# Column sums of the output weights by TensorE from the raw weights, the first z from the keys, token fetches in four pieces

## What is computed

```python
W0 = eye(32)                              # for every sequence and head
def step(W, kv):
    kc, vc = kv
    z = kc @ W                            # the first z is kc itself
    grad = kc.T @ ((z - vc) * inv_n)
    return (W - grad, z)
_, zs = scan(step, W0, (k_chunks, v_chunks))      # 32 chunks
out = (zs - mean(zs)) * rsqrt(var(zs) + eps) * ln_gamma + ln_beta
x = layernorm(x + out @ Wo.T)
```

## Time and profile before

| | |
|---|---|
| median of three runs | 689.74 us |
| the profiled execution | 689.75 us |
| its span | 687.9 us |
| TensorE busy | 662.7 us (96%) |
| VectorE busy | 431.3 us (63%) |
| ScalarE busy | 299.3 us (44%) |
| GpSimd busy | 294.6 us (43%) |

### The profile page before, as it was taken

One profiled execution on the slowest core, in us unless ns is written; L12 is line 12 of the kernel. 1 busy time (PEld: TensorE's weight loads), 2 busy tenths in 40 slices (PEclk: granted clock), 3 DMA queues, 4 the chain that ended last, 5 costly groups with the idle time before them and its releaser, 6 DMA issues.

```text
span 687.9 us, 16521 instructions
## 1 busy us (share of the span) xinstructions
PE 662.7 (96%) x6880; PEld 531.3 (77%) x6880; DVE 431.3 (63%) x750; ACT 299.3 (44%) x520; POOL 294.6 (43%) x308
## 2 busy tenths in 40 slices
PE   9889999999999999999999999999999999999994
PEld 8666777777777777887887888888887888888883
DVE  5796766776844455498956544554456267676555
ACT  5543534445554432431033556655667442142132
POOL 0747657767735531011006335442552244726232
PEclk9999999999999999999999999999999999999998
DMA  8212333331442531100065578666647765414212
GB/s 288 81 35 61 90 106 97 96 111 52 144 139 78 158 114 61 45 1 0 3 244 147 152 286 299 207 228 251 221 159 263 252 191 164 123 65 132 64 77 91
DMA packets 65854, 92.47 MB, mean 134 GB/s; under 512 B 16816, under 2 KB 31920, under 8 KB 65776
## 3 DMA queue, kind: packets, MB, share of 16 engines
q1 hardware_dynamic: 60096, 72.76, 31.8%
q0 software_dynamic: 5680, 18.62, 9.6%
HBM read 67.56 MB, written 23.79 MB: 133 GB/s over the span
## 4 chain that ended last, share of the span: by engine, by line
PE 57%; DVE 20%; POOL 9%; issue 7%; ACT 4%; DMA 2%; DVEq 0%; POOLq 0%; ACTq 0%
PE bank L1311 7%; PE zbank L1274 6%; PE wbank L1274 6%; PE bank L1079 6%; PE zbank L1187 5%; PE bank L1134 5%; PE wbank L1187 4%; PE bank L1200 3%; DVE x L1470 3%; POOL xg L1840 2%; DMA xg<-yd,SI 2%; PE zbank L1287 2%; DVE x L1518 2%; PE bank L1187 2%; PE zbank L1097 2%
## 5 line engine op out<-in xcount | busy, mean ns | idle before, releaser
L1802 POOL TENSOR_TENSOR xl<-RAW,xh 128x1024 fp32r<-128x1024 f32 x23 | 55.4, 2410 | 124.1 <-ACT xh L1669 124.0
L1685 ACT ACTIVATE ah<-sg 128x512 fp32r<-128x512 f32 x48 | 30.3, 632 | 158.9 <-DVE sg L1460 158.9
L1815 POOL DMA_INDIRECT xg<-x1d,idxu x39 | 42.0, 1077 | 70.0 <-DVE idxu L895 41.3
L1450 DVE TENSOR_TENSOR GL<-RAW,GH 128x1024 fp32r<-128x1024 f32 x42 | 50.3, 1223 | 11.0 <-ACT GH L1664 9.6
L1462 DVE TENSOR_TENSOR al<-sg,ah 128x512 fp32r<-128x512 f32 x48 | 35.3, 735 | 33.5 <-ACT ah L1685 33.5
L1200 PE MATMUL bank<-xh,ah 128*128 128x512 f32 x128 | 51.2, 400 | 1.7 <-DVE x L1470 1.1
L1840 POOL DMA_INDIRECT xg<-yd,SI x32 | 34.7, 1086 | 38.1 <-DVE x L1518 23.9
L1200 PE MATMUL bank<-xh,al 128*128 128x512 f32 x128 | 50.0, 390 | 0.0
L1200 PE MATMUL bank<-xl,ah 128*128 128x512 f32 x128 | 49.9, 390 | 0.0
L1079 PE MATMUL bank<-xh,GH 128*128 128x512 f32 x112 | 47.6, 425 | 2.1 <-DVE vst L1366 1.3
L1460 DVE TENSOR_TENSOR sg<-sg,zbank 128x512 f32<-128x512 f32 x22 | 15.1, 685 | 53.3 <-PE zbank L1274 36.4
(11 more groups left out here) (306 smaller groups left out, 1762.3 us busy)
## 6 DMA issues: line engine op xcount, KB each, us to landing
RAW<-in_wgu SPq DMA_DIRECT2D x13, 1024.0 KB, 6.7
yd<-RAW SPq DMA_DIRECT2D x39, 256.0 KB, 4.5
RAW<-in_wsgu SPq DMA_DIRECT2D x14, 512.0 KB, 5.2
RAW<-in_wd SPq DMA_DIRECT2D x13, 512.0 KB, 5.7
xr<-in_xT SPq DMA_DIRECT2D x16, 256.0 KB, 4.6
x<-in_xtok SPq DMA_DIRECT2D x16, 256.0 KB, 3.1
x1d<-x SPq DMA_DIRECT2D x16, 256.0 KB, 2.2
RAW<-in_wsd SPq DMA_DIRECT2D x8, 512.0 KB, 4.5
```

What stands on the lines that cost most here:

```text
L1450: e.tensor_tensor(GL[:, w % 2, k:k + 2, :], gate_raw(w, k), GH[:, w % 2, k:k + 2, :].bitcast(F32), ALU.subtract).then_inc(*mark("low", "g" ...
L1802: e.tensor_tensor(DL[:, w % 2, :, :], draw[:, raw_of(w), :, :], DH[:, w % 2, :, :].bitcast(F32), ALU.subtract).then_inc(*mark("low p", "d" ...
L1815: e.indirect_dma_start(place(s), None, x1d, bass.IndirectOffsetOnAxis(ap=idxu[:, LINES[s]:LINES[s] + 1], axis=0)).then_inc(*mark(f"dma xg{ ...
```

## The change

- The steps `ones`, `wo bias rows`, `wo gamma` and `wo sum` go. A step `wo scales` on ScalarE writes gamma/512 and beta, each repeated over 128 columns, into rows 8 and 9 of `x1`.
- `wo mean` and `wo bias` are four fp32 products each, of those scales with the raw weights. `wo mean` stands directly behind the projections of block 0, `wo bias` directly behind z 1 (they were behind z 1 and behind z 2).
- `wo centre` is one `scalar_tensor_tensor` a quarter, gamma * weights - mean, which reads the mean from PSUM and writes rows 4 to 7 of `x1`; it, `wo high` and `wo low` come two half steps earlier. The copy to `colsum` goes.
- z 0 is no longer multiplied: VectorE takes keys minus values (`first`, 128x256, in `za`) and spreads its first half by the mask; ScalarE spreads the second. The first `v load` and the start copy of `W` go. All four `x high` of block 1 stand behind one another ahead of it.
- `fetch tokens` issues four DMAs of 256 KB; for block 0 two at n = 43 and two at n = 44, with nothing between on SP.
- `rope_of` uses row 11 of `x1` for blocks 1 to 3; `fetch row` 11 waits for key piece (3, 6), 7 and 15 for none, and row 4 for the low output weights.

```diff
-    do("ones")
+    do("wo scales")
...
-    do("wo bias rows")
-    for k in range(4):
-        do("wo gamma", k)
+    do("wo mean", left[6])
     do("w start")
...
-    do("v load", 0)
...
+        do("x high", 1, k, ("proj", 0, 7))
         if k < 2:
-            do("x high", 1, k, ("proj", 0, 7))
             do("x low", 1, k)
...
             if n % 2 == 0:
-                do("z", n // 2)
+                if n:
+                    do("z", n // 2)
                 do("residuals", n // 2)
-                for k in (2, 3) if n == 0 else ():
-                    do("x high", 1, k, ("proj", 0, 7))
...
-        if n == 43:
-            do("fetch tokens", 0, None)
+        if n in (43, 44):
+            do("fetch tokens", 0, None, (2 * n - 86, 2 * n - 85))
...
         if n == 2:
-            do("wo mean", left[7])
-            left[7] = ("wosum", "mean")
-            later.insert(0, [("wo sum", "bias")])
+            do("wo bias", left[7])
+            left[7] = ("wosum", "bias")
+        for k in range(4):
+            if n == 1 + k // 2:
+                do("wo centre", k)
+            if n == 2 + k // 2:
+                do("wo high", k)
+            if n == 3 + k // 2:
+                do("wo low", k)
...
-            return rope if u % 4 == 0 else (kS[:], (zT[:], x1[:, 7, :], x1[:, 15, :], x1[:, 15, :])[q])
+            return rope if u % 4 == 0 else (kS[:], x1[:, 11, :] if q else zT[:])
...
-                    e.dma_start(XL[q % 2][:].bitcast(F32), chunked(x1td[:, q * 512:q * 512 + 512])).then_inc(*mark(f"dma xr{q % 2}", q))
+                    for k in ks:
+                        e.dma_start(XL[q % 2][:, k, :].bitcast(F32), x1td[128 * k:128 * k + 128, q * 512:q * 512 + 512]).then_inc(*mark(f"dma xr{q % 2}", q, k))
...
+                    what, b = ("mean", 6) if step == "wo mean" else ("bias", 7)
+                    e.wait_ge(*on("wo scales"))
+                    e.wait_ge(*on("dma wo"))
                     e.wait_ge(*on(*a[0]))
-                    e.matmul(bank[6][:], onesr[:].bitcast(F32), sums[:, 0, :], start=True, stop=True).then_inc(*mark("sums", "bias"))
+                    for k in range(4):
+                        t = e.matmul(bank[b][:], woscale[b - 6][:, k, :], wor[:, k, :], start=(k == 0), stop=(k == 3))
+                    t.then_inc(*mark("sums", what))
...
-                    e.tensor_tensor(wor[:, k, :], wor[:, k, :], colsum[:], ALU.subtract).then_inc(*mark("woprep", "centre", k))
+                    if k == 0:
+                        e.wait_ge(*on("sums", "mean"))
+                    e.scalar_tensor_tensor(out=woc[:, k, :], in0=wor[:, k, :], scalar=gams[:, k:k + 1], in1=bank[6][:], op0=ALU.mult, op1=ALU.subtract).then_inc(*mark("woprep", "centre", k))
...
+                    if n == 0:
+
+                        e.wait_ge(*on("kturn", 0, 6))
+                        e.wait_ge(*on("vturn", 0, 7))
+                        e.wait_ge(*on("dma small"))
+                        e.tensor_tensor(first.rearrange("p (g x) -> p g x", g=4), KK[:, 0, 1, :].rearrange("p (g x) -> p g x", g=4)[:, :, 0:64],
+                                        vst[0][:, 0, :].rearrange("p (g x) -> p g x", g=4), ALU.subtract).then_inc(*mark("first"))
...
+                elif step == "wo scales":
                     e.wait_ge(*on("dma small"))
-                    for k in range(4):
-                        e.activation(wor[:, k, :], wor[:, k, :], ACT.Copy, scale=gams[:, k:k + 1]).then_inc(*mark("woscaled", "g", k))
+                    for j, (s, c) in enumerate(((gams, 1.0 / 512), (bets, 1.0))):
+                        t = e.activation(woscale[j], s[:].unsqueeze(2).to_broadcast([128, 4, 128]), ACT.Copy, scale=c)
+                    t.then_inc(*mark("wo scales"))
```

More of the change, by code:

```diff
@@ L166, in stages @@
             later.append([("x low", 1, k)])
-    later.append([("wo sum", "mean")])
     def gate(w, q):
@@ L222, in shared @@
         yield from gate(3, 0)
-        do("fetch tokens", 2, ("gate", 3, 0, 1, 1))
+        do("fetch tokens", 2, ("gate", 3, 0, 1, 1), range(4))
         yield from down(2, 1)
@@ L308, in stages @@
         if n == 2:
-            do("wo mean", left[7])
-            left[7] = ("wosum", "mean")
-            later.insert(0, [("wo sum", "bias")])
-        if n == 4:
-            do("wo bias", left[6])
-            left[6] = ("wosum", "bias")
-        for k in range(4):
-            if n == 3 + k // 2:
-                do("wo centre", k)
-            if n == 4 + k // 2:
-                do("wo high", k)
-            if n == 5 + k // 2:
-                do("wo low", k)
+            do("wo bias", left[7])
[7 more added lines that the diff above has]
+                do("wo low", k)
+        if n == 4:
+            left[6] = ("woprep", "centre", 3)
         if n == 34:
@@ L469, in stages @@
         if j == JOBS - 1:
-            do("fetch tokens", 3, row_left[1])
+            do("fetch tokens", 3, row_left[1], range(4))
         if j:
@@ L598, in program @@
         W = part(pa, "late", "W", [2, 256])
-        onesr = part(pa, "late", "onesr", [128], F32R)
         mask = part(pa, "late", "mask", [64])
@@ L604, in program @@
         wgx = part(pa, "late", "wgx", [4, 16], F32R)
-        part(pa, "late", "padl", [176])
+        part(pa, "late", "padl", [304])
         vst = (sb(pa, "vst0", [8, 256]), vst1)
@@ L616, in program @@
         pa.close()
-        wor, wob, sums = x1[:, 12:16, :], x1[:, 4:8, :], x1[:, 8:12, :]
+        first = za[:].rearrange("p m x -> p (m x)")[:, 0:256]
+        wor, woc = x1[:, 12:16, :], x1[:, 4:8, :]
+        woscale = [x1[:, 8 + j, :].rearrange("p (k n) -> p k n", k=4) for j in range(2)]
         rope = (shuf[:], t1[:])
@@ L962, in sync @@
                 elif step == "fetch tokens":
-                    q, after = a
+                    q, after, ks = a
                     if after:
@@ L1371, in vector @@
                         e.tensor_tensor(xl[:, k, :], xr[:, k, :], xh[:, k, :].bitcast(F32), ALU.subtract).then_inc(*mark("low", "x", q, k))
-                elif step == "wo sum":
-                    what, = a
-                    src, at, made = (wor, 2, "g") if what == "mean" else (wob, 0, "b")
-                    e.wait_ge(*on("woscaled", made, 3))
-                    e.tensor_tensor(sums[:, at, :], src[:, 0, :], src[:, 1, :], ALU.add)
-                    e.tensor_tensor(sums[:, at + 1, :], src[:, 2, :], src[:, 3, :], ALU.add).then_inc(*mark("woprep", what, "two"))
-                    e.wait_ge(*on("woprep", what, "two"))
-                    e.tensor_tensor(sums[:, at, :], sums[:, at, :], sums[:, at + 1, :], ALU.add).then_inc(*mark("woprep", what))
                 elif step == "wo centre":
                     k, = a
-                    e.wait_ge(*on("wosum", "mean"))
-                    e.tensor_tensor(wor[:, k, :], wor[:, k, :], colsum[:], ALU.subtract).then_inc(*mark("woprep", "centre", k))
+                    if k == 0:
+                        e.wait_ge(*on("sums", "mean"))
+                    e.scalar_tensor_tensor(out=woc[:, k, :], in0=wor[:, k, :], scalar=gams[:, k:k + 1], in1=bank[6][:], op0=ALU.mult, op1=ALU.subtract).then_inc(*mark("woprep", "centre", k))
                 elif step == "wo low":
@@ L1584, in scalar @@
                     n, = a
+                    r4 = r[:, n // 2 % 2, n % 2, 256:512].rearrange("p (a b e) -> p a b e", a=4, b=2)
+                    if n == 0:
+                        e.wait_ge(*on("first"))
+                        for b in (0, 1):
+                            t = e.activation(r4[:, :, b, :], first[:, 128:256].rearrange("p (a e) -> p a e", a=4), ACT.Copy, scale=mask[:, 32 * b:32 * b + 1])
+                        t.then_inc(*mark("resid a", 0))
+                        continue
                     e.wait_ge(*on("z", n, 1))
@@ L1604, in scalar @@
                     e.activation(xh[:, k, :], xr[:, k, :], ACT.Copy).then_inc(*mark("high", "x", q, k))
-                elif step == "wo mean":
-                    e.wait_ge(*on("sums", "mean"))
-                    e.activation(colsum[:], bank[7][:], ACT.Copy, scale=1.0 / 512).then_inc(*mark("wosum", "mean"))
                 elif step == "wo bias":
                     e.wait_ge(*on("sums", "bias"))
-                    e.activation(bias[:], bank[6][:], ACT.Copy).then_inc(*mark("wosum", "bias"))
+                    e.activation(bias[:], bank[7][:], ACT.Copy).then_inc(*mark("wosum", "bias"))
                 elif step == "wo high":
```

44 lines of the change are left out of this document (12 added, 32 removed).

## The result

The changed kernel takes 688.37 us (median of 20 runs, 687.85 to 689.72), the kernel before on the same chip 690.35 us (20 runs, 689.03 to 693.3): ratio 0.9974, 95% interval 0.9966 to 0.9982. The span of the profiled run fell by 1.4 us.

A forecast was written before the change was run, and what follows sets the result against it. TensorE, nearly full behind 58 us, was taken to bound the kernel, so only waits in front could be won: -0.47, +2.58, +0.43, -1.60, -1.40 and -1.74 sum to -2.2, giving 687.5 us, range 686.3 to 689.4.

The forecast's parts named there:

- The walk through the queue: TensorE's starts carried from 27.81 us to the first output product: 53.27 instead of 55.48, 2.2 us earlier.
- the reason given: At z 2: ScalarE's W copy queues behind the bias copy until 42.3 us, so z 2 waits some 0.4 us.
- The 0.43 us a record: In both sums on TensorE: fp32 records start 0.43 us apart, eight taking 3.44 us; upper bound 0.53 apart.
- The cover of the mean sum: Behind block 0's projections: the mean costs little, lying where TensorE waited; g 0 still 0.47 us earlier.
- the bias sum in the path: Behind z 1: four products instead of one stand fully in the path, making g 1 2.1 us later than before.
- Pieces at nothing: Token fetches in four issues cost nothing; the last has 3.2 us of cover, the other two more.
- pieces land later: Rival at the token fetches: a second spread of 2.8 us passes the cover, leaving +0.2, 689.9 us; chance 0.06.
- VectorE's sizes: In front: keys minus values at most 0.42 us, low output weights at most 2.34 a pair; no wait at g 0.
- reaches the end almost whole: Behind the first 58 us TensorE is nearly full, so the 2.2 us earlier start carries to the end.
- a stall goes as well: Rival inside z at 183.06 us: TensorE's 0.91 us standstill vanishes too; -3.1, 686.6 us; chance 0.10.
- bytes and place are the same: Argument against the 0.91 us standstill at 183.06 us vanishing: the first 1 MB fetch keeps its bytes and place.
- given back: Rival behind 58 us: a VectorE or GpSimd step loses its slack, half the gain lost; -1.0, 688.7 us; chance 0.14.

The follow-up runs named there:

- experiment 7: The changed kernel with two of the mean sum's four fp32 products left out; 688.0 us, ratio 0.9964 to the kernel before.
- experiment 8: The changed kernel with two of the bias sum's four fp32 products left out, which changes routing and expert tiles; 684.35 us, ratio 0.9917 to the kernel before.
- experiment 3: The changed kernel with each token fetch as one DMA again; 688.61 us, ratio 0.9963 to the kernel before.
- 1: The changed kernel run again unaltered for a second trace; 688.56 us, ratio 0.9972 to the kernel before.
- 9: The changed kernel with its bias sum two steps later, behind g 2; 690.19 us, ratio 1.0004 to the kernel before.
- 10: The changed kernel with its warm-up of ten fp32 products made 5 wide and 31 narrow, 52 records more; 688.95 us, ratio 0.9986 to the kernel before.
- 11: The changed kernel with its warm-up of ten fp32 products made 7 wide and 16 narrow, 26 records more; 688.76 us, ratio 0.9983 to the kernel before.
- 12: The changed kernel with 13 narrow fp32 products added ahead of the x1 turn near 214 us; 688.69 us, ratio 0.9982 to the kernel before.
- experiment 4: The kernel before with only the first z taken from the keys; 690.28 us, ratio 1.0 to the kernel before.
- 5: The kernel before with the first z from the keys and four unused fp32 products ahead of the projections; 689.89 us, ratio 0.9997 to the kernel before.
- 6: The changed kernel with z 0 multiplied as before and one DMA per fetch, column sums alone; 689.08 us, ratio 0.9975 to the kernel before.

## Why the prediction was right

**The walk through the queue** came out within 0.12 us at every step: the mean's end (31.3 forecast; the second projection behind it starts at 31.56, which is 31.33 and one spacing), g 0 at 32.80 (32.75), z 1 at 35.16 (35.13), g 1 at 39.58 (39.55), z 2 at 42.47 (42.35) with its wait of 0.46 (0.4) for the reason given, g 2 at 46.20 (46.13), g 3 at 50.93 (50.89), the output product at 53.21 (53.27). The 0.43 us a record, the term with the widest bounds, held: 0.86 a product, where the four passes of the Trainium skill that the prediction names would give 0.91.

**The cover of the mean sum** was right (experiment 7), and **the bias sum in the path** too (experiment 8). **Pieces at nothing**: right (experiment 3); they landed 3.1 to 8.1 us behind their issues, the whole fetches 5.2 to 8.0. The section of the Trainium skill that the rival "pieces land later" names gives its 2 us for transfers issued by GpSimd; these are issued by SP.

**VectorE's sizes were wrong, and hidden.** The difference of keys and values took 1.34 us, not at most 0.42, and the first pair of low weights 3.48, not at most 2.34. VectorE's half of the residual of g 0 was ready at 32.1 and ScalarE's at 32.4 (31.5 forecast), ahead of 32.80, and that of z 2 at 44.6, ahead of 46.2, so no start moved; that 0.4 us were left at g 0 was luck. The step that failed is the choice of the rows for the bounds. GpSimd was busy in both: the row of 0.42 lies within its pair of subtractions, but that operation reads `zbank`, which is PSUM, and the new one reads keys and values, both in SBUF. The row of 2.34 ran beside one GpSimd operation, the new pair beside two.

```profile
53.05 1.74 POOL L1775 TENSOR_TENSOR zst<-za,vst 128x512 f32<-128x512 f32 x1
```

**What the prediction did not see** lies behind the front. That the shift "reaches the end almost whole" holds by the medians (2.0 of 2.2 us), but in the profiled pair -2.27 became -1.43, and in the second trace of the change -2.24 became -1.60. So that the end agrees is in part luck: what was lost at 282 us and at the jump was partly made up by the gain at 180 us and, in the medians, by runs of the kernel before that read 0.6 above its profiled one. Of the rival "a stall goes as well", the stall did go, but its reason against, "bytes and place are the same", missed that the place in TensorE's list was not the same, and only 0.4 of its 0.9 showed since a wait for ScalarE lay under it. Of the rival "given back", 0.37 went at 282 us and 1.1 at the jump. The first did go to a VectorE step, but one that starts late, not one that lost its slack; the second is a stand of TensorE's own that depends on the count of instructions ahead. The loss at 282 us (after, and experiments 1, 3, 7, 8, 9 and 10 to 12, not 4, 5 and 6) is open in its cause. In all nine traces that show it VectorE's multiplication starts 0.85 us behind the product, in the five others 0.50, whatever the lead; the nine have both halves of the change, and with them 345 VectorE instructions ahead of that one, where the others have 344, 350 or 351.

Why the list's place makes TensorE stand was varied by no run alone, but the traces point at the supply of instructions. The profile lists a DMA queue of kind "instruction" (56 packets, 0.92 MB, so 16 KB each). The kernel before has 6880 records of products and 6880 of weight loads, which would be 246 a packet, and where TensorE only runs products of 0.227 us the packets start 28 to 29 us apart (563.4, 592.7, 621.3, 649.6), the time of some 126 products with their loads. That the queue is TensorE's is an estimate from these numbers. In all five traces with the stand in the z, the stand ends 2.2 to 2.3 us behind the start of a packet (183.06 behind 180.80 before), while its length goes from 0.54 to 1.91 us, and this packet starts 9.6 to 11.9 us behind its forerunner. The changed kernel's starts 7.3 us behind its own, at 178.84, 3.3 us before the place is reached. All eight stands at the jump end 2.5 to 2.8 us behind a packet. So TensorE most likely waits for its next instructions, whose packet comes late. What makes it late, the token fetch ahead of it (DMA share 0.99 to 1.03 from 176 to 180 us before) or something else, is not shown.

## What to carry over

When a front is bound by waits of TensorE for a slower engine, walk its queue start to start and put the added work where it waits; the same work one step later, outside the hole, costs most of its length (1.37 of 1.72 us in experiment 8). A removed piece may need its hole filled: look at the granted clock behind every gap. And a change of a few dozen instructions moves TensorE's own stands of 0.4 to 1.9 us elsewhere: with a gain of 2 us, compare leads place by place and not only the ends.

## What the runs showed of the hardware

- **The clock fell behind a half-empty stretch, but not behind every one.** Busy 2.06 of 4 us, then 0.50 for some 3.5 us (experiment 4); with the fillers 1.00 throughout (5); busy 1.97 of the same 4 us in the kernel before, and 1.00 throughout. After a stand of 1.9 us it was 0.50 from 183 to 186 us (10). Products of 128x512 then follow each other by 0.43 us. The Trainium skill (TensorE: Matmul & The Clock Gate, Part 1) knows two levels, by how busy the array has recently been, and 426.7 ns for such a product at the lower; the trace agrees.
- **VectorE stands behind GpSimd.** An operation of 128x256 with both inputs in SBUF took 1.34 us from 30.30 to 31.64 while GpSimd's second subtraction ran to 31.37, and 0.42 for the same size when GpSimd was idle; a pair of 128x512 took 3.48 under GpSimd and 1.25 without. With one input in PSUM 128x256 took 0.42 under GpSimd too (at 30.24 before). The Trainium skill (SBUF — State Buffer, SBUF: two separate sides) says that such an operation and a GpSimd one that reads SBUF lock each other out for a whole instruction. The trace agrees: 31.37 and some 0.3 is 31.64.
- **Stands of TensorE that hang on its place in its list**, released by no engine's work that the profile shows: 0.5 to 1.9 us in the z, moved record by record by instructions ahead of it (6, 10, 11), and 0.4 to 0.9 us at the jump, gone with 26 records more ahead (11, 12). They end 2.2 to 2.8 us behind the start of a packet of the queue "instruction".
- **A narrow fp32 product of full height costs more than a small one**: 0.036 us a record for 128 rows by 32 columns (12) against 0.013 for the 32-row ones, 64 of which take 0.85 us.
